# Two reorderings in an eight-core attention and router-LoRA layer: one engine per step in the last normalization drain, and the router's transposes ahead of the LoRA-A matmuls

## The reference

```python
x = layernorm(x + attn(x, Wqk, Wv, Wo))            # 8 heads of 64, softmax / sqrt(512)
xf = x.reshape(-1, 4096)
logits = xf @ W_router.T                           # 8 experts
probs = softmax(logits)
topk_p, topk_i = top_k(probs, 2); topk_p /= topk_p.sum(-1)
combine = sum(one_hot(topk_i, 8) * topk_p)         # tokens x 8
h = einsum('nd,erd->ner', xf, A_stack) * combine[..., None]
lora = einsum('ner,eor->no', h, B_stack) * 2.0
x = layernorm(xf + xf @ W_base.T + b_base + lora)
```

## Time and profile before

| | |
|---|---|
| timed runs, median (lowest to highest) | 4137.7 us (4105.95 to 4169.45, 2 runs) |
| profiled execution, its own time | 3984.23 us |
| its span, slowest core (all cores) | 3982.7 us (3928.7 to 3982.7) |
| busy PE, DVE, ACT, POOL | 81%, 32%, 22%, 17% of the span |
| mean granted TensorE clock of that core | 0.83 of full |

### The profile page before, as it was taken

How to read it: one execution, slowest core, us unless ns; L and a number is a source line. 1 busy time by engine, 2 the same in 40 slices (tenths; PEclk the granted TensorE clock), 3 DMA queues, 4 the chain that set the end, 5 groups by cost and what they waited for, 6 DMA issues and landing times.

```text
span 3982.7 us, 46555 instructions; the slowest of 8 cores (3928.7 to 3982.7 us)
## 1 busy us (share of the span) xinstructions
PE 3206.1 (81%) x13476; PEld 1183.7 (30%) x13476; DVE 1291.9 (32%) x1972; ACT 863.9 (22%) x1476; POOL 668.0 (17%) x543
## 2 busy tenths in 40 slices
PE   4667699778998989899888986614999998999950
PEld 2555234221221222222222221101444433444420
DVE  1000100125555565555556348831000011111124
ACT  1222000002443344444434432200000000000000
POOL 1111000000000000000000015542222213444425
PEclk7999799885776576776778689956999998999975
DMA  7999644520000000000000033216454535776637
GB/s 224 277 281 285 182 135 135 180 85 6 6 6 14 6 6 1 14 6 6 1 19 6 1 100 109 85 63 208 127 160 144 157 132 173 205 208 209 203 112 190
DMA packets 451794, 444.79 MB, mean 112 GB/s; under 512 B 22624, under 2 KB 403681, under 8 KB 451554
## 3 DMA queue, kind: packets, MB, share of 16 engines
q1 hardware_dynamic: 348642, 341.13, 29.4%
q10 hardware_dynamic: 102912, 100.68, 7.9%
HBM read 340.01 MB, written 100.66 MB: 111 GB/s over the span
## 4 chain that ended last, share of the span: by engine, by line
PE 58%; DVE 8%; issue 5%; DMA 4%; POOL 3%; ACT 1%; SPq 0%; DVEq 0%; POOLq 0%; ACTq 0%
PE pf L155 25%; PE sS L155 11%; PE rb L155 9%; PE a L155 7%; DVE racc L629 4%; DMA res2d<-r2scr 2%; POOL tmpf L1035 2%; PE po L155 2%; DVE x2g L1046 1%; POOL tmpo L1186 1%; PE sS L654 1%; PE pss L155 1%; PE psq L155 1%; DVE res L981 1%; PE pstS L155 1%
## 5 line engine op out<-in xcount | busy, mean ns | idle before, releaser
L155 PE MATMUL pf<-x2h,wqf 128*128 128x512 bf16 x4096 | 910.0, 380 | 5.8 <-DVE hs L1382 5.8
L629 DVE TENSOR_REDUCE racc<-sS 128x1 f32<-128x512 f32 x1024 | 682.1, 689 | 506.0 <-PE sS L155 495.3
L777 ACT ACTIVATE probs<-rb 128x512 bf16<-128x512 f32 x1024 | 540.9, 597 | 754.5 <-PE rb L155 754.1
L155 PEld LDWEIGHTS pf<-x2h,wqf 128*128 128x128 bf16 x4096 | 396.7, 98 | 505.9 <-issue 39.6
L155 PE MATMUL sS<-kT,qT 64*128 64x512 bf16 x1024 | 480.9, 489 | 75.7 <-DVE racc L629 38.9
L155 PE MATMUL pk<-xbf,wk_bf 128*128 128x256 bf16 x2048 | 266.5, 283 | 146.2 <-ACT xbf L367 60.3
L155 PE MATMUL a<-probs,V 128*65 128x512 bf16 x1024 | 374.8, 492 | 0.0
L1407 POOL CAST wqf<-wstgf 128x1024 bf16<-128x1024 f32 x256 | 264.6, 1040 | 594.4 <-DMA wstgf<-wbT 427.6
L1473 DVE SCALAR_TENSOR_TENSOR res2c<-pf,bB_sb,x2h 128x1024 bf16<-128x1024 f32 x64 | 82.2, 1284 | 865.0 <-PE pss L155 793.3
L155 PE MATMUL rb<-qT,kT 64*128 64x512 bf16 x1024 | 343.4, 479 | 0.2
L589 POOL CAST wo_bf<-wstgo 128x1024 bf16<-128x1024 f32 x16 | 16.6, 1040 | 1727.0 <-DMA wstgo<-woT 1727.0
(11 more groups left out here) (107 smaller groups left out, 1675.2 us busy)
## 6 DMA issues: line engine op xcount, KB each, us to landing
wstgf<-wbT SPq DMA_DIRECT2D x256, 512.0 KB
xstg<-xrot SPq DMA_DIRECT2D x128, 512.0 KB
xscr<-xbf ACTq DMA_DIRECT2D x128, 256.0 KB, 5.6
xvb<-xscr SPq DMA_DIRECT2D x128, 256.0 KB, 2.7
outT<-outst ACTq DMA_DIRECT2D x64, 512.0 KB, 4.9
xqb<-xscr SPq DMA_DIRECT2D x32, 512.0 KB, 3.9
xq<-xscr SPq DMA_DIRECT2D x32, 512.0 KB, 3.8
x2scr<-x2g ACTq DMA_DIRECT2D x32, 512.0 KB, 2.8
```

The source lines that it names most:

```text
L155: return lambda e: e.matmul(o, l, r, start=st, stop=sp, skip_group_check=True)
L629: e.reduce_max(d, srd, AX.X, negate=True),
L777: e.activation(d, srd, AF.Exp),
```

## The change

It has two parts. In the last group of the output projection the odd chunks are applied as the even ones are: POOL multiplies, DVE adds. And the eight transposes of the router's logits, with their copies, are issued ahead of the LoRA-A matmuls instead of behind them.

```diff
-                            def mk_apply(mc=mc, qg=qg):
+                            def mk_apply(mc=mc):
                                 def f():
                                     ti = mc % 2
-                                    t1 = s.op("DVE" if qg == 3 and mc % 2
-                                              else "POOL",
+                                    t1 = s.op("POOL",
                                               lambda e, d=tmpf[ti][:],
...
-                                    t2 = s.op("POOL" if qg == 3 and mc % 2
-                                              else "DVE",
+                                    t2 = s.op("DVE",
                                               lambda e,
                                               d=x2g[:, mc * 512: mc * 512 + 512],
...
                     lg8R.did_write(tlg)
+                    for qc in range(8):
+                        tt = s.op("PE",
+                                  lambda e, o=pf[1].ap()[0:128, 0:8],
+                                  i=lg8[:, qc * 128: qc * 128 + 128],
+                                  idn=id32[0:8, 0:8]: e.transpose(o, i, idn),
+                                  waits=lg8R.rd() + pfR[1].wr())
+                        lg8R.did_read(tt)
+                        pfR[1].did_write(tt)
+                        tc = s.op("DVE", lambda e, d=lgt[:, qc * 8: qc * 8 + 8],
+                                  srd=pf[1].ap()[0:128, 0:8]: e.tensor_copy(d, srd),
+                                  waits=[tt] + (lgtR.wr() if qc == 0 else []))
+                        pfR[1].did_read(tc)
+                        lgtR.did_write(tc)
                     w0 = pfR[0].wr()
                     last = None
                     for dc in range(NDC):
...
                     t_loraA = last
-                    for qc in range(8):
-                        tt = s.op("PE",
...
-                        lgtR.did_write(tc)
```

## The result

| | before | with the change |
|---|---|---|
| median of the timed runs | 3998.07 us (27 runs) | 3966.97 us (28 runs) |
| ratio of the times | | 0.9939, 95% interval 0.991 to 0.9968 |
| profiled execution, its own time | 3984.23 us | 3958.69 us |
| its span, slowest core | 3982.7 us | 3957.1 us |

Single executions of either kernel lie between 3937 and 4274 us, and the slow ones, over 1.5% above the fastest of their kernel or with a die at a lower clock, are left out of the ratio; the two runs of before that stood ahead of the prediction, 4106 and 4169 us, are among them.

What follows compares the result with a forecast made beforehand. Matmuls on PE hold 58% of the chain; the change touches only stretches where PE waits. Drain 11.3 plus router halves 5.6 and 3.2 make 20.1 us saved: 4117.6 from a median of 4137.7, range 3960 to 4150.

Steps and rivals of the forecast that it cites:

- The drain: Last group of the output projection: POOL multiplies, DVE adds, 52.8 us instead of 64.1, so 11.3 us saved.
- The router: LoRA-A behind the logit transposes covers PE's wait for `cmb`; 5.6 us saved in half 0, 3.2 in half 1.
- The charge for the clock: Router: small transposes ahead lower PE's clock, so LoRA-A gets 2.3 us longer in each half.
- The restart of 11.5 us: Router, upper bound of the clock's cost: clock back only after 11.5 us, so 5.7 us lost per half.
- From the `cmb` transposes on all is as before: Router behind LoRA-A: nothing changes, with the clock low at the start of the base matmuls in both kernels.
- The low clock throughout: Rival, router: all 64 LoRA-A matmuls at 1.2 GHz, 28 us instead of 14; 3.3 us lost, 4141; chance 0.05.
- no holding up: Rival, drain: the engines do not delay each other, drain 37.8 us; 35.1 us saved in all, 4102.6; chance 0.09.
- a router that gives nothing: Rival: something else, a weight tile or `x2h`, ends last before the base matmuls; 11.3 us saved, 4126.4; chance 0.06.
- Full exclusion: Rival, drain: no multiplication beside an addition, 3.70 us a pair, drain 59.2; 13.7 us saved in all, 4124; chance 0.10.
- On their median of 4137.7 it gives 4117.6: Whole kernel: the 20.1 us saved, taken off the median of the timed runs of before, gives the predicted time.
- the mechanisms' own 4098 to 4141: Whole kernel: span of times that the mechanisms alone give, before widening for the spread between executions.
- within 2%: Verdict for the whole kernel: a change below 2% (83 us) has nearly everything; 0.06 left for faster, 0.04 for slower.

Runs made afterwards that it cites:

- e5: The changed kernel with four buffers for the product (tmpf) instead of two; one profiled execution took 3931.79 us, the drain 50.4 us.
- e3: The changed kernel with the addition's second operand read straight from PSUM and the copy bbc dropped; ratio to the kernel before 0.9792 (0.9713 to 0.9872).
- e4: The changed kernel with the eight logit transposes spread through the first half of LoRA-A, one behind every four matmuls; ratio to the kernel before 0.9945 (0.9902 to 0.9988).

## Why the prediction was right in its terms, and where it failed

**The drain, right.** 52.8 us were forecast from the spacing of pairs in the earlier groups, 52.7 came. The same two instructions in another place of the same trace were the best price to be had; the simple sum, 32 x 1.16 + 0.69, would have missed by 15 us.

**The router, right.** LoRA-A at 14.0 + 2.3 = 16.3 us was forecast, 16.6 and 16.5 came; 5.6 and 3.2 us saved, 5.5 and 3.1 came. The charge for the clock, taken from the restart of the base matmuls, was needed: without it the two halves would have been overrated by the 2.6 and 2.5 us that LoRA-A got longer. The restart of 11.5 us, the other bound, did not come. One reading there was wrong, though the bound did not hang on it: "busy PE stayed low for 11.5 us" holds for the granted clock, 0.50 until 3292; PE itself was busy in full from 3282 on.

**A small term put at nothing.** "From the `cmb` transposes on all is as before" left out that the clock would be high again behind LoRA-A: it still was for the first three and the first seven of these transposes (0.27 us each instead of 0.37), and the two halves got 0.3 and 0.7 us shorter from there.

**The rivals.** The low clock throughout, no holding up and a router that gives nothing all fall by the rows above. *Full exclusion* I had set against my forecast, at 3.70 us a pair. Here the step failed that took the solo lengths, 1.16 and 0.69, as the time for which an instruction keeps the other out. e5 and e3, with the one-sided stretching in the drain, show that the engines do exclude each other, and that this still lets a pair pass in 3.1 us when they take turns without a pause; the part of an instruction that keeps the other out is shorter than the length that the profile gives it (1.16 + 0.69 is 1.85 us, and one of each passes every 1.56). So the 3.29 us of the rows were no evidence against exclusion; the rival and the forecast were one mechanism, and the rival's price was wrong.

**The level and the verdict, wrong.** Two steps failed here. "On their median of 4137.7 it gives 4117.6" put the saving on two runs; 27 runs have their median at 3998, and the profiled execution's 3984, which I had set aside for the level, was the typical one. 3964, the other number of the sum, lies 3 us from the measured 3967. That 3967 still lies in the range is luck: the mechanisms' own 4098 to 4141 misses it, and only the widening to 3960 for the spread between executions took it in. And "So 'within 2%' has nearly everything" treated a saving that the sum itself put at 20 us as no change, because 2% was taken for "about what a measurement of this kernel can tell from no change". With 28 runs against 27 the measurement tells 0.6% from none: 13 to 36 us, with the forecast 20 and the 21.0 of the books well inside. The mechanisms and their sum were clear of nothing at both bounds (4.3 to 39.7 saved), and that, not the 2%, was what the verdict should have rested on.

## What to carry to other kernels

When POOL and DVE are to work side by side, look in the trace for an instruction that lasts well beyond its solo time (here 1.5 to 1.6 us instead of 0.69): the wait sits inside it, and no semaphore shows it. Give DVE's operation only one SBUF input (here the other came from PSUM) before dividing work between the two engines; by the stages that was worth some 66 us, three times the 21 of the reordering. Small PE work that has to wait for round trips is better put between the matmuls of a long stretch than ahead of it; here that took 3.4 and 5.9 us off the two halves, by the stages alone.

## What the runs showed that I had not expected

- The exclusion reaches far beyond the drain: with the addend in PSUM the three groups that run beside the output projection went from 79.3 to 62.7 us each, some 50 us together, against 16 us in the drain.
- With four buffers the block vanishes from the waits of the two engines and appears as longer instructions (1.57 instead of 1.16 us on POOL, 1.60 instead of 0.69 on DVE), while the drain hardly changes: 50.4 against 52.7 us.
- Half 0's clock fell in e4 during LoRA-A's own matmuls, about a microsecond after an idle wait of 2.12 us had ended, and was back by 2736. It fell so on five of the eight cores there, and on core 6 of the kernel before. What in the stretch before it decides this, no run here separates.
